# Three PNA layers of a graph network: batch norm folded into the mix weights, layer norm on ScalarE, the next head in groups of five blocks

## The chip, the cores and the metric

One core of one Trainium2 chip runs the kernel. The metric is the device time of one launch in microseconds (us), the median of three runs. Engines: PE (TensorE), DVE (VectorE), ACT (ScalarE), POOL (GpSimd), and SP, which here only issues DMAs.

## What is computed

A graph of N = 3125 nodes and 50000 edges, sorted by destination, with D = 128 features a node (float32), passes four parts: GCN, GIN, SAGE and three PNA layers, each part added to its input and layer-normed. The change lies in the PNA layers:

```python
def _pna_layer(h, src, dst, Mw, Mb, Uw, Ub, bn_g, bn_b, mix_w, mix_b):
    msg = jnp.concatenate([h[src], h[dst]], axis=-1) @ Mw.T + Mb
    ...            # sums of msg and msg*msg, max and min of msg over each node's edges
    agg = jnp.concatenate([mx, mn, std, var], axis=-1)
    ...            # h_neigh: agg, and agg scaled twice by the logarithm of the degree
    u = jnp.concatenate([h, h_neigh], axis=-1) @ Uw.T + Ub
    u = u * jnp.sqrt(1.0 / N)
    mu = jnp.mean(u, axis=0)
    v = jnp.mean((u - mu) ** 2, axis=0)
    u = (u - mu) / jnp.sqrt(v + BN_EPS) * bn_g + bn_b
    out = jax.nn.leaky_relu(u @ mix_w.T + mix_b, 0.01)
    return out + h
for l in range(3):
    h = _pna_layer(h, src_sl, dst_sl, Mw[l], ...)
    mu, v = ...    # mean and variance of each node's row
    h = jax.nn.elu((h - mu) / jnp.sqrt(v + LN_EPS) * ln_g[l] + ln_b[l])
```

## The kernel before

The nodes lie in NB = 25 blocks of 128, in NG = 5 groups of GB = 5 blocks; NCB = 7 banks hold four blocks each. There is no scheduler: each engine has its own program, written out by hand, in which every wait on a semaphore stands in its place, so the order on an engine is the order of the code. A layer runs like this.

**Head.** When a group of x is ready (s_grp), PE turns the blocks one by one (L1524) into two banks in turn, ACT copies each to ft2 or ft (L1318), PE multiplies it by M (L1621), DVE copies the result to g (L976). g is the part of the message that depends on the source node. Ahead of that, DVE writes the first four slots of source indices (L968). SP then writes g to DRAM as a_dram (L491, one DMA of 1600 KB) and starts two slabs of the count matrix (L456). DVE makes ft = g * g (L979) and splits g and ft into three bf16 parts each (L774 and L779, casts on ACT at L1211 and L1217).

**Loop.** POOL waits for a_dram and gathers rows by source index (L615): one gather per column of edges, four columns a slot (Q = 4), four slots (RING), so 16 in a batch. DVE runs the maximum and minimum over the columns (L1045, L1048), and writes the next indices for a slot when it has used it; between two batches it takes one block's share of PE's sums (L991 to L1024). SP writes the columns' state to scan_dram (L502). After the last column POOL gathers the ends of the segments from scan_dram (L632).

**U products, batch norm.** PE turns the ends and multiplies them by U (L1689, L1697), DVE adds up (L1112 to L1114), PE turns the result so that edge_sum holds u with features on the partitions (L1705), DVE takes statistics and makes cscale and cshift (L845 to L850).

**Mix.** For each block ACT makes turned = edge_sum * cscale + cshift (L1374), PE multiplies it by the mix weights (L1709) and adds the bias as a product of one row of ones with the bias row (L1710), ACT copies the bank to agg (L1379). A float32 product shows in the trace as a pair of passes. After a group DVE takes the leaky maximum (L1126), adds x (L1127) and takes row statistics (L1129); after all, L1132, the root on ACT (L1249) and rstd (L1135).

**Layer norm and ELU.** DVE subtracts the mean and multiplies by the first row of weights block by block (L1140), then by rstd and adds the second row (L1144). ACT makes exp(-relu(-y)) of a group in g (L1385, L1387); DVE takes max(y, 0) - 1 (L1151) and adds g, which gives x (L1152, s_grp). These two are one group behind. Weights of the next layer are loaded by SP as soon as the last use of the old ones is over (s_y). After the third layer x3 is reloaded (L521), added and normed (L828 to L837), and written out (L523, L525).

## Time and profile before

| | |
|---|---|
| median of three runs | 3907.63 us (3900.43 to 3912.53) |
| the profiled execution | 3915.32 us |
| its span | 3913.5 us |
| PE busy | 2472.3 us (63%) |
| DVE busy | 2233.6 us (57%) |
| POOL busy | 1258.7 us (32%) |
| ACT busy | 692.3 us (18%) |
| mean granted TensorE clock | 0.785 |

The span runs from the first to the last instruction that the profile shows; the execution's own time holds 1.8 us more. Busy times are of the whole span, whose last 2500 us, roughly, are the three PNA layers. The clock is given as a share of full speed (2.4 GHz).

### The profile page before, as it was taken

How to read it: one execution, taken by the hardware profiler on the slowest of the kernel's cores; microseconds unless marked ns; L12 is line 12 of the kernel's file. 1: busy time of each engine (PE TensorE's matmuls, PEld its weight loads, DVE VectorE, ACT ScalarE, POOL GpSimd, SP SyncE). 2: the span in 40 equal slices, each digit the busy share in tenths (PEclk: the TensorE clock that was granted, in tenths of full speed). 3: DMA queues.
4: the chain of work that ended last, by engine and by line, in shares of the span. 5: the costliest groups of instructions: out<-in, count | busy, mean ns of one | idle time of the engine just before them, and what ended most of it. 6: DMA issues, size and time to landing. Idle time of an engine off the chain costs nothing. (4 is left out here: it accounts for less than half of the span.)

```text
span 3913.5 us, 50857 instructions
## 1 busy us (share of the span) xinstructions
PE 2472.3 (63%) x11996; PEld 1384.5 (35%) x11997; DVE 2233.6 (57%) x6995; ACT 692.3 (18%) x1557; POOL 1258.7 (32%) x1321
## 2 busy tenths in 40 slices
PE   6988879886968955455456654454448644544563
PEld 2444345743635532222224422222225322222242
DVE  6877766463353265555555645555556645555555
ACT  0235532411121030000001500000003300000112
POOL 3000000002000036666642155655640356555520
PEclk8999989997979977677678676766767867767785
DMA  3122366253523535444441144444430444444411
GB/s 109 50 93 109 142 210 230 99 206 124 176 81 138 176 100 179 159 163 159 138 145 40 53 160 144 160 155 135 157 113 1 141 136 160 154 134 158 153 43 45
DMA packets 152225, 511.54 MB, mean 131 GB/s; under 512 B 32194, under 2 KB 51552, under 8 KB 151248
## 3 DMA queue, kind: packets, MB, share of 16 engines
q1 hardware_dynamic: 94782, 350.03, 25.5%
q0 software_dynamic: 43536, 93.43, 8.6%
q10 hardware_dynamic: 13826, 67.12, 4.2%
q8 instruction: 37, 0.61, 0.1%
q14 instruction: 44, 0.36, 0.0%
HBM read 280.33 MB, written 230.13 MB: 130 GB/s over the span
## 5 line engine op out<-in xcount | busy, mean ns | idle before, releaser
L615 POOL DMA_INDIRECT rows_g<-a_dram,idx_now x1173 | 1133.3, 966 | 1566.8 <-DMA a_dram<-g 801.4
L1485 PE MATMUL psum<-hs,slab 128*128 128x384 bf16 x6600 | 1196.2, 341 | 166.2 <-issue 124.0
L1485 PEld LDWEIGHTS psum<-hs,slab 128*128 128x128 bf16 x6600 | 674.5, 102 | 711.2 <-issue 326.3
L1045 DVE SCALAR_TENSOR_TENSOR run<-run,mask_pt,rows_g 128x128 f32<-128x128 f32 x1170 | 405.6, 347 | 278.5 <-issue 224.7
L1048 DVE SCALAR_TENSOR_TENSOR run<-run,mask_pt,rows_g 128x128 f32<-128x128 f32 x1170 | 403.3, 345 | 34.6 <-issue 26.8
L1637 PE MATMUL psum<-identity,std_now 128*128 128x128 f32 x75 | 33.6, 448 | 598.1 <-ACT std_now L1341 512.9
L1432 PE MATMUL psum<-onehot_key,onehot_lane 128*128 128x512 bf16 (+1 forms) x1968 | 366.4, 343 | 60.9 <-issue 36.3
L726 DVE TENSOR_SCALAR onehot_key<-key_row,key_at 128x1600 bf16<-128x1600 f16 x492 | 310.2, 630 | 0.0
L1644 PE MATMUL psum<-w_U,vturned 128*128 128x384 f32 x150 | 119.2, 896 | 292.6 <-ACT vturned L1349 265.2
L1341 ACT ACTIVATE std_now<-var_now,eps 128x128 f32<-128x128 f32 x75 | 30.1, 401 | 1444.5 <-DVE var_now L1007 928.9
L1432 PEld LDWEIGHTS psum<-onehot_key,onehot_lane 128*128 128x128 bf16 x1968 | 160.4, 100 | 249.5 <-issue 55.0
L1637 PEld LDWEIGHTS psum<-identity,std_now 128*128 128x128 f32 x75 | 13.2, 176 | 629.9 <-ACT std_now L1341 536.9
L804 DVE TENSOR_REDUCE agg<-psum 128x384 f32 (+1 forms) x125 | 69.5, 556 | 271.3 <-PE psum L1505 240.4
L725 DVE TENSOR_SCALAR onehot_lane<-lane_row,lane_at 128x128 bf16<-128x128 f16 x492 | 123.8, 252 | 103.3 <-PE psum L1432 86.1
L797 DVE SCALAR_TENSOR_TENSOR run<-run,var_tmp 128x128 f32<-128x128 f32 x391 | 137.4, 351 | 59.3 <-DVE run L797 15.7
L1644 PEld LDWEIGHTS psum<-w_U,vturned 128*128 128x128 f32 x150 | 36.3, 301 | 320.7 <-ACT vturned L1349 292.6
L603 POOL DMA_INDIRECT edge_sum<-sums_dram,end_idx x25 | 23.8, 953 | 388.6 <-DMA sums_dram<-run 381.3
L593 POOL PARTITION_ALL_REDUCE most<-most x1 | 0.4, 380 | 440.7 <-DVE most L744 440.7
L991 DVE TENSOR_REDUCE var_tmp<-psum 128x128 f32<-128x384 f32 x150 | 76.4, 551 | 76.7 <-remote 54.8
L1697 PE MATMUL psum<-w_U,turned 128*128 128x384 f32 x300 | 115.3, 509 | 0.1
L1185 ACT ACTIVATE part_now<-psum 128x1600 bf16<-128x1600 f32 x50 | 74.9, 1499 | 191.6 <-PE psum L1453 170.9
L1645 PE MATMUL psum<-w_U,vturned 128*128 128x384 f32 x150 | 107.2, 817 | 0.0
(298 smaller groups left out, 3018.2 us busy)
## 6 DMA issues: line engine op xcount, KB each, us to landing
slab<-at_part SPq DMA_DIRECT2D x200, 800.0 KB
scan_dram<-run SPq DMA_DIRECT2D x291, 512.0 KB
at_part<-part_now ACTq DMA_DIRECT2D x50, 800.0 KB, 3.6
sums_dram<-run ACTq DMA_DIRECT2D x43, 576.0 KB, 2.9
rows_g<-a_dram,idx_now POOLq DMA_INDIRECT x1173
rows_g<-in_attr SPq DMA_DIRECT2D x43, 148.5 KB
a_dram<-g SPq DMA_DIRECT2D x3, 1600.0 KB, 7.7
agg<-sel_dram SPq DMA_DIRECT2D x3, 1600.0 KB
```

Source lines behind the costliest of these rows:

```text
L615: nc.gpsimd.indirect_dma_start(rows_g[:, slot, j, :], None, a_dram, bass.IndirectOffsetOnAxis(ap=idx_now[:, slot, j:j + 1], axis=0)).then_ ...
L725: V.tensor_scalar(onehot_lane[:, j, :], lane_row[:], lane_at[:, ds(at, 1)], None, ALU.is_equal)
L726: V.tensor_scalar(onehot_key[:, j, :], key_row[:], key_at[:, ds(at, 1)], None, ALU.is_equal).then_inc(s_oh, 1)
L797: V.scalar_tensor_tensor(esum[:, slot, j, :], before, same[:, ds(EC * e + j, 1)], esum[:, slot, j, :], ALU.mult, ALU.add).then_inc(s_erun, 1)
L991: last = V.tensor_reduce(var_tmp[:, k, :], bank(2 + 2 * odd + k)[:, 0:3 * D].rearrange("p (s f) -> p f s", s=3), AX.X, ALU.add)
L1045: V.scalar_tensor_tensor(at[:, 0:D], before[:, 0:D], mark, rows, ALU.add, ALU.max).then_inc(s_run, 1)
L1048: V.scalar_tensor_tensor(at[:, D:2 * D], before[:, D:2 * D], mark, rows, ALU.subtract, ALU.min).then_inc(s_run, 1)
L1432: mm = T_.matmul(psum[:, 2048 * h + lo:2048 * h + hi], onehot_lane[:, j, :], onehot_key[:, j, lo:hi], start=(start and j == 0), stop=False ...
L1485: T_.matmul(ps[:, 0:3 * D], counts[:, k * P:(k + 1) * P], hs[:, k, at:at + 3, :].rearrange("p s f -> p (s f)"), start=(k == 0), stop=False ...
L1644: T_.matmul(bank(7)[:, 0:3 * D], vturned[:, 0:P], weights["U"][:, 2, :], start=True, stop=False)
L1645: T_.matmul(bank(7)[:, 0:3 * D], vturned[:, P:2 * P], weights["U"][:, 3, :], start=False, stop=True).then_inc(s_vmm, 1)
L1697: mm = T_.matmul(bank(2 + b % 2)[:, 0:3 * D], turned[:, b % 2, j * P:(j + 1) * P], weights["U"][:, j, :], start=(j == 0), stop=(j == 1))
```

## The change

It does four things.

- **Mix.** u * cscale + cshift, times the mix weights, is u times (cscale * weights), plus a row that is the same for all nodes. DVE scales the weights once (mix_now), PE makes cshift times the weights as one row, DVE adds the bias (mix_row). PE then multiplies edge_sum as it is, four blocks into a bank, and adds the row to the whole bank with one product of 512 columns. ACT writes 0.01 times the bank to agg, one operation a bank; DVE takes the maximum of that and the bank, adds x, and takes statistics.
- **Layer norm.** ACT normalizes each block (scale rstd, bias minus_mean); DVE multiplies and adds the two weight rows for a group of five blocks at once.
- **Head.** The next layer's transposes, copies and M products are done by groups of five blocks and written between the groups of the norm on all three engines (take_g, copy_xt). Layer 0 has them ahead of its loop. The first index slots are written ahead of the norm.
- **DMAs.** a_dram is written in five pieces, POOL waits for all of them. The weights of the next layer but M are loaded behind these and ahead of the slabs; those loads whose values no layer uses are left out.

```diff
+                for i in range(NG):
+                    sp.wait_ge(s_g, NG * l + i + 1)
+                    sp.dma_start(a_dram[GB * i * P:(GB * i + GB) * P, :].rearrange("(b p) f -> p b f", p=P),
+                                 g[:, GB * i:GB * i + GB, :]).then_inc(s_a_out, 16)
+                if l == 0:
+                    sp.wait_ge(s_x3, 16)
+                    sp.wait_ge(s_sel_out, 16)
+                else:
+                    sp.wait_ge(s_y, NG * l)
+                    layer_weights(LATER, l, s_lw)
                 load = counts(l + CALLS, 2)
                 load(0, 0, 0)
                 load(1, 1, 0)
...
-                layer_weights(["M"], (l + 1) % LAYERS, s_lm)
-                sp.wait_ge(s_y, NG * l + NG)
-                layer_weights(LATER, (l + 1) % LAYERS, s_lw)
+                if l + 1 < LAYERS:
+                    layer_weights(["M"], l + 1, s_lm)
...
-                pool.wait_ge(s_a_out, 16 * l + 16)
+                pool.wait_ge(s_a_out, 16 * NG * l + 16 * NG)
...
+            def take_g(l, i):
+
+                dve.wait_ge(s_gm, NG * l + i + 1)
+                at = 2048 + 1024 * (i % 2)
+                V.tensor_copy(flat(g)[:, GB * D * i:GB * D * (i + 1)], psum[:, at:at + GB * D]).then_inc(s_g, 1)
+
+            def first_indices(l):
+
+                if l:
+                    dve.wait_ge(s_run, 2 * T * l)
+                for k in range(RING):
+                    V.tensor_copy(idx_now[:, k, :], src_pt[:, Q * k:Q * k + Q]).then_inc(s_idx, 1)
+
+            def told_by(ins_):
+
+                made[0] += 1
+                ins_.then_inc(s_dve, 1)
+                return made[0]
+
+            first_indices(0)
+            for i in range(NG):
+                take_g(0, i)
...
-                if l:
-                    dve.wait_ge(s_run, 2 * T * l)
-                for k in range(RING):
-                    take_indices(0, k)
-                for b in range(NB):
-                    dve.wait_ge(s_mm, 3 * NB * l + MM3 + (b + 1))
-                    V.tensor_copy(g[:, b, :], bank(4 + b % 2)[:, 0:D]).then_inc(s_res, 1)
-                dve.wait_ge(s_res, 2 * NB * l + MM3 + NB)
+                dve.wait_ge(s_g, NG * l + NG)
...
                 batch_norm(lcols[:, 0:1], lcols[:, 1:2], S_LAYER * l + (S_X3 + 1))
-                for i in range(NG):
-                    at = slice(GB * i, GB * i + GB)
-                    dve.wait_ge(s_res, 2 * NB * l + (MM3 + NB + GB * i + GB))
-                    step(V.scalar_tensor_tensor(agg[:, at, :], agg[:, at, :], 0.01, agg[:, at, :], ALU.mult, ALU.max))
-                    step(V.tensor_tensor(agg[:, at, :], agg[:, at, :], x[:, at, :], ALU.add))
-                    for b in range(GB * i, GB * i + GB):
-                        last = V.bn_stats(stats[:, b, :], agg[:, b, :])
-                step(last)
+                V.tensor_scalar(mix_now[:], weights["mix"][:], cscale[:, 0:1], None, ALU.mult).then_inc(s_mix_now, 1)
+                dve.wait_ge(s_shifted, l + 1)
+                V.tensor_tensor(mix_row[:], bank(7)[0:1, 0:D], lrows[0:1, 2, :], ALU.add).then_inc(s_mix_row, 1)
+
+                def stats_of(j):
+                    for b in range(4 * j, min(NB, 4 * j + 4)):
+                        ins_ = V.bn_stats(stats[:, b, :], agg[:, b, :])
+                    return ins_
+
+                for j in range(NCB):
+                    at = slice(4 * j, min(NB, 4 * j + 4))
+                    rows, ps = agg[:, at, :], bank(j)[:, 0:(at.stop - at.start) * D].rearrange("p (b f) -> p b f", f=D)
+                    dve.wait_ge(s_leak, NCB * l + j + 1)
+                    leaky = told_by(V.tensor_tensor(rows, rows, ps, ALU.max))
+                    if j:
+                        stats_of(j - 1)
+                    dve.wait_ge(s_dve, leaky)
+                    added = told_by(V.tensor_tensor(rows, rows, x[:, at, :], ALU.add))
+                    dve.wait_ge(s_dve, added)
+                step(stats_of(NCB - 1))
                 for b in range(NB):
                     last = V.bn_aggr(mv[:, b, :], stats[:, b, :])
                 last.then_inc(s_rows, 1)
                 dve.wait_ge(s_std, S_LAYER * l + (S_X3 + 2))
                 step(V.reciprocal(rstd[:], std[:]))
-                for i in range(NG + 1):
+                V.scalar_tensor_tensor(minus_mean[:], mv[:, :, 0], -1.0, rstd[:], ALU.mult, ALU.mult).then_inc(s_rstd, 1)
+                if l + 1 < LAYERS:
+                    first_indices(l + 1)
+
+                def on_group(k):
+                    return lrows[:, k:k + 1, :].to_broadcast([P, GB, D])
+
+                for i in range(NG + 2):
+                    now, past = slice(GB * i, GB * i + GB), slice(GB * i - GB, GB * i)
                     if i < NG:
-
-                        for b in range(GB * i, GB * i + GB):
-                            last = V.scalar_tensor_tensor(agg[:, b, :], agg[:, b, :], mv[:, b, 0:1], lrows[:, 3, :],
-                                                          ALU.subtract, ALU.mult)
-                        step(last)
-                        for b in range(GB * i, GB * i + GB):
-                            last = V.scalar_tensor_tensor(agg[:, b, :], agg[:, b, :], rstd[:, b:b + 1],
-                                                          lrows[:, 4, :], ALU.mult, ALU.add)
-                        last.then_inc(s_y, 1)
-                    if i >= 1:
-
-                        at = slice(GB * i - GB, GB * i)
+                        dve.wait_ge(s_norm, NG * l + i + 1)
+                        scaled = told_by(V.tensor_tensor(agg[:, now, :], agg[:, now, :], on_group(3), ALU.mult))
+                    if 1 <= i <= NG:
                         dve.wait_ge(s_e, NG * l + i)
-                        step(V.tensor_scalar(agg[:, at, :], agg[:, at, :], 0.0, -1.0, ALU.max, ALU.add))
-                        V.tensor_tensor(x[:, at, :], agg[:, at, :], g[:, at, :], ALU.add).then_inc(s_grp, 1)
+                        upper = told_by(V.tensor_scalar(agg[:, past, :], agg[:, past, :], 0.0, -1.0, ALU.max, ALU.add))
+                    if i < NG:
+                        dve.wait_ge(s_dve, scaled)
+                        V.tensor_tensor(agg[:, now, :], agg[:, now, :], on_group(4), ALU.add).then_inc(s_y, 1)
+                    if 1 <= i <= NG:
+                        dve.wait_ge(s_dve, upper)
+                        V.tensor_tensor(x[:, past, :], agg[:, past, :], g[:, past, :], ALU.add).then_inc(s_grp, 1)
+                    if i >= 2 and l + 1 < LAYERS:
+                        take_g(l + 1, i - 2)
...
+            def copy_xt(l, i):
+
+                act.wait_ge(s_xt, NG * l + i + 1)
+                at = 1024 * (i % 2)
+                A.copy(ft2[:, GB * P * i:GB * P * (i + 1)], psum[:, at:at + GB * P]).then_inc(s_xc, 1)
+
+            for i in range(NG):
+                copy_xt(0, i)
...
-                act.wait_ge(s_rows, told(4))
-                for i in range(NB + 1):
-                    if i < NB:
-                        if i >= 2:
-                            act.wait_ge(s_mm, mms + (2 * NB + i - 1))
-                        A.activation(turned[:, i % 2, 0:D], edge_sum[:, i, :], ACT.Identity, bias=cshift[:, 0:1],
-                                     scale=cscale[:, 0:1]).then_inc(s_trc, 1)
-                    if i >= 1:
-                        b = i - 1
-                        act.wait_ge(s_mm, mms + (2 * NB + b + 1))
-                        A.copy(agg[:, b, :], bank(4 + b % 2)[:, 0:D]).then_inc(s_res, 1)
+                for j in range(NCB):
+                    at = slice(4 * j, min(NB, 4 * j + 4))
+                    act.wait_ge(s_mixed, NCB * l + j + 1)
+                    A.mul(agg[:, at, :], bank(j)[:, 0:(at.stop - at.start) * D].rearrange("p (b f) -> p b f", f=D),
+                          0.01).then_inc(s_leak, 1)
                 root_of(told(5), std[:], mv[:, :, 1], 0)
+                act.wait_ge(s_rstd, l + 1)
+
+                def normalize(i):
+
+                    for b in range(GB * i, GB * i + GB):
+                        last = A.activation(agg[:, b, :], agg[:, b, :], ACT.Identity, bias=minus_mean[:, b:b + 1],
+                                            scale=rstd[:, b:b + 1])
+                    last.then_inc(s_norm, 1)
+
+                normalize(0)
                 for i in range(NG):
-
+                    if i + 1 < NG:
+                        normalize(i + 1)
                     at = slice(GB * i, GB * i + GB)
                     act.wait_ge(s_y, NG * l + (i + 1))
                     A.activation(g[:, at, :], agg[:, at, :], ACT.Relu, scale=-1.0).then_inc(s_neg, 1)
                     act.wait_ge(s_neg, NG * l + (i + 1))
                     A.activation(g[:, at, :], g[:, at, :], ACT.Exp, scale=-1.0).then_inc(s_e, 1)
+                    if i >= 1 and l + 1 < LAYERS:
+                        copy_xt(l + 1, i - 1)
+                if l + 1 < LAYERS:
+                    copy_xt(l + 1, NG - 1)
...
+                for i in range(NG + 1):
+                    if i < NG:
+                        pe.wait_ge(s_grp, NG * l + (i + 1))
+                        if i >= 2:
+                            pe.wait_ge(s_xc, NG * l + (i - 1))
+                        for j in range(GB):
+                            at = 1024 * (i % 2) + j * P
+                            mm = T_.transpose(psum[:, at:at + P], x[:, GB * i + j, :], identity[:])
+                        mm.then_inc(s_xt, 1)
                     if i >= 1:
-                        b = i - 1
-                        pe.wait_ge(s_trc, trcs + (b + 1))
-                        if b >= 2:
-                            pe.wait_ge(s_res, ress + (b - 1))
-                        T_.matmul(bank(4 + b % 2)[:, 0:D], ft2[:, b * P:(b + 1) * P], weights["M"][:, 0:D],
-                                 start=True, stop=True).then_inc(s_mm, 1)
+                        k = i - 1
+                        pe.wait_ge(s_xc, NG * l + (k + 1))
+                        if k >= 2:
+                            pe.wait_ge(s_g, NG * l + (k - 1))
+                        for j in range(GB):
+                            at, b = 2048 + 1024 * (k % 2) + j * D, GB * k + j
+                            mm = T_.matmul(psum[:, at:at + D], ft2[:, b * P:(b + 1) * P], weights["M"][:, 0:D],
+                                          start=True, stop=True, skip_group_check=True)
+                        mm.then_inc(s_gm, 1)
+                pe.wait_ge(s_g, NG * l + NG)
...
-                def mixed(ps, t):
-                    T_.matmul(ps[:, 0:D], t, weights["mix"][:], start=True, stop=False)
-                    return T_.matmul(ps[:, 0:D], ones[0:1, :], weights["L3_rows"][0:1, 2, :], start=False, stop=True)
-
-                turned_products(None, 3 * NB * l + 7 * NB, 2 * NB * l + (MM3 + NB), mixed)
+                T_.matmul(bank(7)[0:1, 0:D], cshift[:], weights["mix"][:], start=True, stop=True).then_inc(s_shifted, 1)
+                pe.wait_ge(s_mix_now, l + 1)
+                for j in range(NCB):
+                    blocks = range(4 * j, min(NB, 4 * j + 4))
+                    for b in blocks:
+                        T_.matmul(bank(j)[:, (b - 4 * j) * D:(b - 4 * j + 1) * D], edge_sum[:, b, :], mix_now[:],
+                                 start=(b == 4 * j), stop=False, skip_group_check=True)
+                    if j == 0:
+                        pe.wait_ge(s_mix_row, l + 1)
+                    T_.matmul(bank(j)[:, 0:len(blocks) * D].rearrange("p (b f) -> p b f", f=D), ones[0:1, :],
+                             mix_row[:].unsqueeze(1).to_broadcast([1, len(blocks), D]), start=False, stop=True,
+                             skip_group_check=True).then_inc(s_mixed, 1)
```

PE, start of the mix stage (turned is ACT's result, w_L_rows the bias row). Before:

```order
L1705 MATMUL psum<-identity,u_row 128x128 [waits s_act,s_u] x2
L1709 MATMUL psum<-w_mix,turned 128x128 [waits s_trc,s_rows]
L1710 MATMUL psum<-w_L_rows,ones 128x128
L1709 MATMUL psum<-w_mix,turned 128x128 [waits s_trc]
L1710 MATMUL psum<-w_L_rows,ones 128x128
L1709 MATMUL psum<-w_mix,turned 128x128 [waits s_res,s_trc]
```

Now:

```order
L1780 MATMUL psum<-identity,u_row 128x128 [waits s_act,s_u] x2
L1782 MATMUL psum<-w_mix,cshift 1x128 [waits s_rows]
L1787 MATMUL psum<-mix_now,edge_sum 128x128 [waits s_mix_now]
L1787 MATMUL psum<-mix_now,edge_sum 128x128 x3
L1791 MATMUL psum<-mix_row,ones 128x512 [waits s_mix_row]
L1787 MATMUL psum<-mix_now,edge_sum 128x128 x4
L1791 MATMUL psum<-mix_row,ones 128x512
```

A bias product followed each block; now one follows four blocks, and no bank waits for a copy.

DVE, end of the norm and start of the next layer's head. Before:

```order
L1140 SCALAR_TENSOR_TENSOR agg<-agg,mv,w_L_rows 128x128 x5
L1144 SCALAR_TENSOR_TENSOR agg<-agg,rstd,w_L_rows 128x128 [waits s_dve]
L1144 SCALAR_TENSOR_TENSOR agg<-agg,rstd,w_L_rows 128x128 x4
L1151 TENSOR_SCALAR agg<-agg 128x640 [waits s_e]
L1152 TENSOR_TENSOR x<-agg,g 128x640 [waits s_dve]
L1151 TENSOR_SCALAR agg<-agg 128x640 [waits s_e]
L1152 TENSOR_TENSOR x<-agg,g 128x640 [waits s_dve]
L968 COPY idx_now<-src_pt 128x4 [waits s_run,s_grp]
L968 COPY idx_now<-src_pt 128x4 x3
L976 COPY g<-psum 128x128 [waits s_mm] x25
```

Now, from the third group of the norm on:

```order
L1194 TENSOR_TENSOR agg<-agg,w_L_rows 128x640 [waits s_norm]
L1197 TENSOR_SCALAR agg<-agg 128x640 [waits s_e]
L1200 TENSOR_TENSOR agg<-agg,w_L_rows 128x640 [waits s_dve]
L1203 TENSOR_TENSOR x<-agg,g 128x640 [waits s_dve]
L986 COPY g<-psum 128x640 [waits s_gm]
L1194 TENSOR_TENSOR agg<-agg,w_L_rows 128x640 [waits s_norm]
```

The 25 copies of g behind the norm have become five, the first three of them between the groups of the norm, each with a wait on PE; the ten small operations a group have become two large ones.

## Rows read from the trace of the kernel before

**Rows 1.** Windows, end of layer 0: span, each engine's busy time and count, clock, DMA

```profile
2151.00:2188.00 37.00, 35.59 (x100) 24.54 (x100) 11.23 (x31) 16.50 (x50) 0.00 (x0) 0.52 0.00 1
2214.00:2227.00 13.00, 12.71 (x73) 9.85 (x72) 7.53 (x30) 5.95 (x23) 0.00 (x0) 0.86 0.14 52
```

**Rows 2.** Timeline of DVE: start, length (us), operation, [idle before <- releaser]

```profile
1411.84 3.48 DVE L979 TENSOR_TENSOR ft<-g 128x3200 f32<-128x3200 f32 x1
...
2151.16 0.16 DVE L850 TENSOR_TENSOR cshift<-w_L_cols,cshift 128x1 f32<-128x1 f32 x1
...
2189.64 1.07 DVE L1129 BATCH_NORM_STATS2 stats<-agg 128x6 f32<-128x128 f32 x5
...
2192.88 0.32 DVE L1135 RECIPROCAL rstd<-std 128x25 f32<-128x25 f32 x1 [0.39 <-ACT std L1249]
...
2213.15 0.83 DVE L1152 TENSOR_TENSOR x<-agg,g 128x640 f32<-128x640 f32 x1
...
2227.04 3.48 DVE L979 TENSOR_TENSOR ft<-g 128x3200 f32<-128x3200 f32 x1
...
2282.47 1.02 DVE L991 TENSOR_REDUCE var_tmp<-psum 128x128 f32<-128x384 f32 x2 [17.79 <-remote]
```

**Rows 3.** Timeline of POOL and DVE, start of the loops of layers 1 and 2

```profile
2235.64 2.44 POOL L615 DMA_INDIRECT rows_g<-a_dram,idx_now  x1 [145.98 <-DMA a_dram<-g]
...
2245.87 2.74 DVE L779 TENSOR_TENSOR hs<-agg,hs 128x640 bf16<-128x640 f32 x3 [0.47 <-ACT hs L1217]
...
2277.29 0.94 POOL L615 DMA_INDIRECT rows_g<-a_dram,idx_now  x1 [0.30 <-issue]
...
3079.31 2.74 DVE L779 TENSOR_TENSOR hs<-agg,hs 128x640 bf16<-128x640 f32 x3 [0.47 <-ACT hs L1217]
...
3110.83 0.94 POOL L615 DMA_INDIRECT rows_g<-a_dram,idx_now  x1 [0.30 <-issue]
...
3115.86 1.02 DVE L991 TENSOR_REDUCE var_tmp<-psum 128x128 f32<-128x384 f32 x2 [18.43 <-remote]
```

**Rows 4.** Timeline of POOL: two batches of layer 1's loop, first gathers of the ends

```profile
2058.69 0.94 POOL L632 DMA_INDIRECT hs<-scan_dram,end_idx  x1 [26.61 <-DMA scan_dram<-run]
...
2500.55 0.94 POOL L615 DMA_INDIRECT rows_g<-a_dram,idx_now  x1 [7.01 <-DVE idx_now L968]
...
2526.74 0.94 POOL L615 DMA_INDIRECT rows_g<-a_dram,idx_now  x1 [6.37 <-DVE idx_now L968]
...
2893.02 0.94 POOL L632 DMA_INDIRECT hs<-scan_dram,end_idx  x1 [13.43 <-DMA scan_dram<-run]
```

**Rows 5.** Timeline of PE: passes of an earlier part, and layer 0's first transposes

```profile
682.27 0.42 PE L1524 MATMUL psum<-identity,agg 128*128 128x128 f32 x1
682.49 1.91 PE L1557 MATMUL psum<-turned,w_L_W1T 128*128 128x128 f32 x8
...
685.52 0.27 PE L1524 MATMUL psum<-identity,agg 128*128 128x128 f32 x1
685.63 1.06 PE L1557 MATMUL psum<-turned,w_L_W1T 128*128 128x128 f32 x8
...
1089.81 1.10 PE L1592 MATMUL psum<-ft,w_L_W 128*128 128x512 f32 x2 [0.28 <-DVE ft L926]
...
1397.41 0.69 PE L1524 MATMUL psum<-identity,x 128*128 128x128 f32 x2 [10.88 <-DVEq L767]
```

**Rows 6.** Timeline of ACT: the first two operations of the mix stage

```profile
2151.36 0.88 ACT L1374 ACTIVATE turned<-edge_sum,cshift,cscale 128x128 f32<-128x128 f32 x2 [0.81 <-DVE cshift L850]
```

**Rows 7.** Groups by line, 1750 to 3913: count | busy, mean ns | idle before

```profile
L1385 ACT ACTIVATE g<-agg 128x640 f32<-128x640 f32 x15 | 11.1, 737 | 32.9 <-DVE agg L1144 32.9
...
L1151 DVE TENSOR_SCALAR agg<-agg 128x640 f32<-128x640 f32 x15 | 7.3, 490 | 1.2 <-ACT g L1387 0.9
```

**Rows 8.** DMA issues, 2210 to 2250: count, KB each, median us to landing

```profile
a_dram<-g SPq DMA_DIRECT2D x1, 1600.0 KB, 7.7
...
w_L_rows<-in_L_rows SPq DMA_DIRECT2D x1, 320.0 KB, 4.3
```

More of the change, by code:

```diff
@@ L175, in gnn_kernel @@
         cshift = sb("cshift", [P, 1], F32)
+        mix_now = sb("mix_now", [P, D], F32)
+        mix_row = sb("mix_row", [1, D], F32)
+        minus_mean = sb("minus_mean", [P, NB], F32)
         eps = sb("eps", [P, 2], F32)
@@ L343, in gnn_kernel @@
         s_res = sem("s_res")
+        s_xt = sem("s_xt")
+        s_xc = sem("s_xc")
+        s_gm = sem("s_gm")
+        s_g = sem("s_g")
+        s_mix_now = sem("s_mix_now")
+        s_shifted = sem("s_shifted")
+        s_mix_row = sem("s_mix_row")
+        s_mixed = sem("s_mixed")
+        s_leak = sem("s_leak")
+        s_rstd = sem("s_rstd")
+        s_norm = sem("s_norm")
         s_hid = sem("s_hid")
@@ L525, in _ @@
             sp.dma_start(out[(NB - 1) * P:N, :], x[0:N - (NB - 1) * P, NB - 1, :]).then_inc(s_out, 16)
-            sp.wait_ge(s_lm, 16 * (LAYERS + 1))
-            sp.wait_ge(s_lw, 16 * len(LATER) * (LAYERS + 1))
+            sp.wait_ge(s_lm, 16 * LAYERS)
+            sp.wait_ge(s_lw, 16 * len(LATER) * LAYERS)
             sp.wait_ge(s_out, 32)
@@ L1313, in told @@
                     return V_LAYER * l + V_X3 + k
-                mms = 3 * NB * l + MM3
-                for b in range(NB):
-                    act.wait_ge(s_tr, 2 * NB * l + 4 * NB + (b + 1))
-                    A.copy(ft2[:, b * P:(b + 1) * P], bank(b % 2)[:, 0:P]).then_inc(s_trc, 1)
+                mms = NB * l + MM3
                 taken, turns = [0], [0]
@@ L1609, in _ @@
                 pe.wait_ge(s_lm, 16 * l + 16)
[L1610 to L1622 removed]
+                trcs = NB * l + 5 * NB
+                for i in range(NG + 1):
[7 more added lines that the diff above has]
+                        mm.then_inc(s_xt, 1)
+                    if i >= 1:
+                        k = i - 1
[8 more added lines that the diff above has]
+                pe.wait_ge(s_g, NG * l + NG)
                 for b in range(NB):
```

20 lines of the change are left out of this document (5 added, 15 removed).

## Prediction

> **What bounds the kernel now.** I read the page first. Its chain of waits covers only a few per cent of the span, so it can't say what a stage is worth. I cut the boundary between two layers of the last part into stretches instead [rows 1]: while the mix products run, PE is busy 35.6 of 37 us at a granted clock of 0.52; during the head of the next layer (transposes, M products) it is busy 12.7 of 13 us. Next I took DVE's timeline across the same boundary [rows 2]. The batch norm's shift is ready at 2151.3, the last statistics end at 2190.7, rstd at 2193.2, the last x at 2214.0, the last g at 2227.0. These stand behind one another: the reader should see three stages in series, 39.4, 20.8 and 13.0 us. They run on one path, once per layer.
>
> After g the path is less plain. DVE has 22 us of splits and then 18 us in which it waits at L991 until 2282.5 [rows 2]. POOL starts its gathers at 2235.6, when a_dram has landed, and runs 32 in a row to 2278.2; DVE goes on 4.2 us later. In the next layer the last of the 32 ends at 3111.8 and DVE goes on at 3115.9, 4.1 us later [rows 3]. In the loop the same shape returns: POOL pauses for 6 to 7 us after a batch of 16 gathers, and the batches start 26.2 us apart [rows 4]. So I take it that the loop hangs on POOL: what starts POOL earlier moves the layer. The splits have over 10 us of slack.
>
> **The mix products.** Before: 25 blocks, each a pair of passes for the product and a pair for the bias, 0.72 us a pair at the low clock (35.6 us for 100 passes) [rows 1]. Streams of 128-column passes without the change between 128 and 1 rows start 0.22 us apart at the low clock and 0.11 at the high one (682.27 to 682.49 and 685.52 to 685.63, and the runs of 8 behind them); a pair of 512 columns takes 1.10 less its last pass's end, 0.85, at the high clock, so 1.7 at the low [rows 5]. The change makes 25 product pairs and 7 bias pairs (six of 512 columns). Low clock: 4 x 0.44 + 1.7 + some 0.5 for two switches = 4.0 a bank, 25.4 in all. High clock: 2.2 a bank on PE, and now DVE sets the pace: the maximum and the sum over 512 elements (0.69 each, 0.83 being that of 640), four statistics 0.85 [rows 2] and waits give 2.4 a bank. With 0.5 us for the shift product and the row ahead, and about 2.1 us behind PE for the last bank, the stage takes 28.0 us low; high it is 0.5 + 2.2 + 0.6 (ScalarE's first bank) + 6 x 2.4 + 1.7 = 19.4. Against 39.4: **-11.4 or -20.0**. ScalarE's 50 small operations become 7 and are covered by PE.
>
> Which clock? Before, this stage stayed at 1.2 GHz for 36 us although PE was 96% busy; half of its passes feed one row. The head beside it, all on 128 rows, rose to 2.4 GHz within its 13 us (mean 0.86) [rows 1]. The new stage streams more densely, 43% of the time on 128 rows, and lies between. I take the middle, **-15.7**, and keep both ends.
>
> *A page against the row.* The Trainium skill (TensorE: Matmul & The Clock Gate, "What's actually happening") says the clock is set by how busy PE has recently been. By that the old stage should have run at full clock; its row says 0.52, and the measurement decides. If the page's rule were all there is, the new stage would rise and the high value would hold.
>
> **Norm, ELU and the next head.** Before, 20.8 + 13.0 = 33.8 us from rstd to g. Now ScalarE normalizes (5 x 0.39 a group, the pitch of the pair at L1374 [rows 6]), DVE scales and shifts whole groups (2 x 0.83), ELU's two steps 0.49 + 0.83 [rows 2, 7], and DVE then takes a head group (0.83) that waits for PE: five transposes of the group just finished and five products of the one before. That is a new wait, and queued behind it on DVE is the next group's scaling. PE's part is 3.6 us low (5 x 0.22 and 10 x 0.22, a start each) and 1.9 high. A full round is 3.0 + 0.8 + 3.6 + 0.1 = 7.5 us low, 5.8 high. I walked the three engines through: the first g group is taken 16.3 us (14.6) after rstd, the next ones start at 23.8 (20.3), 31.2 (26.0), 37.1 (30.2), 39.4 (31.4), end 40.3 (32.2). With 0.3 for the negated mean: 40.6 or 32.5, **+6.8 or -1.3**. PE now has short bursts with pauses, so neither clock is sure: middle +2.8. ScalarE (1.95 + 0.74 + 0.74 [rows 7] + 0.7 = 4.1 a group, and one table load) stays under the round. So the overlap gives nearly nothing: ScalarE and PE trade with DVE in turn.
>
> **a_dram in five pieces.** Before, 1600 KB land after 7.7 us [rows 8] and POOL starts 8.7 us after the last g [rows 2, 3]. Now only 320 KB are left. Bounds: a 320 KB load behind 768 KB took 4.3 us [rows 8]; a fifth of 7.7 is 1.5. With 1.0 for the way to POOL I take 3.5, nearest to the proportion: **-5.2** (-3.4 to -6.2). POOL's 17th gather needs the indices that DVE makes after the first columns, 23.6 us after g; POOL would want them 3.5 + 20.4 = 23.9 after g, so just in time. The weights of the next layer move on SP's queue from before the head to behind the five pieces and ahead of the two slab loads; even at a landing time of 4.3 us [rows 8] for that queue they hide behind the 22 us of splits.
>
> **Layer 0 and the end.** Layer 0's head took 14.4 us, 1397.4 to 1411.8 [rows 5, 2]. Nothing else is in its way now; PE's five groups need 11.3 us (low for the first 4.5), the last copy 0.9: -2, and -5.2 for POOL: **-7.2**. The last layer has no head: the norm loses 1.3 us (22.1 for 20.8: group 1's ELU waits for two normalizations and the table), the mix gains 15.7, and the weights that nobody uses no longer precede the load of x3, 0.5: **-14.9**.
>
> **Sum.** Two boundaries at -15.7 + 2.8 - 5.2 = -18.1, so -36.2; -14.9; -7.2: **-58.3 us**. The profiled execution is 3915.3 us, 7.7 above the median of 3907.6; the sum gives 3857 there and **3850** against the median. The indices at the loop's start, the new row and column tiles and the semaphores are hidden (DVE's four copies lie beside ScalarE's first group); without that cover 0.4 us a layer.
>
> **Rivals.**
> - *Clock high in both stages* (busy is enough). -20.0 - 1.3 - 5.2 = -26.5 twice, -19.2, -7.2 = -79: 3828. For it: the denser stream. Against: 36 us at 0.52. The rule of the Trainium skill's page above would give this outcome; the trace disagrees so far.
> - *Clock low in both*. -9.8 twice, -10.6, -7.2 = -37: 3870. For it: the row-poor bias passes stay 1.7 us long.
> - *POOL's start isn't what the loop waits for.* DVE goes on 33.9 us after the splits' end in layer 1 and 33.8 in layer 2 [rows 2, 3], which fits as well as POOL's 4.2 and 4.1. Then the three 5.2 are not gained: 3865. Against it: in the loop each batch of POOL is followed by the same release.
> - *Slower: the loop's period grows.* From g to the first gather of the ends, layer 0 takes 646.9 us and layer 1 666.0 [rows 2, 4], with the same code and idle time that the profile calls issue: 19.1 us, 0.8 for each of 24 batches. The change moves all code behind it. One more such step in every layer costs layer 0 38.2 us and the others 19.1 each, 76.4 in all: 3926. It decides from there: below 70 us (1.0 a batch over 72) the result is no slower than before. The other way, layers 1 and 2 at layer 0's pace give 3812.
> - *The change doesn't do what it says*: DVE blocked at the first g group could stall more than I walked. At +29 us a boundary it cancels the gain; each of four rounds would have to take some 15 us instead of 7.5.
>
> **Chances.** Forecast 0.40, high clock 0.16, low clock 0.16, POOL not the bound 0.12, short loops 0.05, long loops 0.07, cancelled 0.04; each spills a little over its edge. The likeliest gives 3850; 3815 to 3890 takes in both clocks and the two ends of the a_dram price. A measurement of this kernel tells about 0.3% (12 us) from no change; faster 0.87, same 0.05, slower 0.08.
>
> **What would show it.** In the profile after: the mix stage 19 to 28 us from shift to last statistics, its clock above 0.52 where the middle holds; copies of g at DVE five times a layer with a wait on PE of 2 to 4 us before each; POOL starting 3 to 4 us after the last of them; DVE's release at L991's successor 46 to 47 us after POOL's start; the batches 25 to 26.5 us apart. I am wrong if the release stays 34 us behind the splits while POOL starts earlier, if POOL's batches drift apart, or if the rounds exceed 8 us.

## The result, and the profile after

| | before | after |
|---|---|---|
| median | 3905.24 us (3900.43 to 3912.53, 4 runs) | 3847.77 us (3835.11 to 3856.43, 4 runs) |
| ratio, 95% interval | | 0.9851 (0.983 to 0.9871) |
| span of the profiled execution | 3913.5 us | 3854.6 us |
| PE / DVE / ACT / POOL busy | 2472.3 / 2233.6 / 692.3 / 1258.7 us | 2450.6 / 2204.9 / 673.8 / 1263.9 us |
| mean granted TensorE clock | 0.785 | 0.785 |

The change takes 57.5 us off the median; 3850 was forecast. The spans differ by 58.9 us, the sum of the prediction was 58.3. So good an agreement of totals has to be checked stage by stage.

Timeline of DVE after the change, from the end of layer 0 on (start, length, operation, [idle before <- releaser]):

```profile
2142.16 0.16 DVE L869 TENSOR_TENSOR cshift<-w_L_cols,cshift 128x1 f32<-128x1 f32 x1
...
2170.33 1.76 DVE L1179 BATCH_NORM_AGGREGATE mv<-stats 128x2 f32<-128x6 f32 x25
2172.47 0.32 DVE L1182 RECIPROCAL rstd<-std 128x25 f32<-128x25 f32 x1 [0.39 <-ACT std L1302]
...
2188.42 0.82 DVE L986 COPY g<-psum 128x640 f32<-128x640 f32 x1 [3.43 <-PE psum L1694]
2189.16 0.81 DVE L1194 TENSOR_TENSOR agg<-agg,w_L_rows 128x640 f32<-128x640 f32 x1
2189.89 0.49 DVE L1197 TENSOR_SCALAR agg<-agg 128x640 f32<-128x640 f32 x1
2190.30 0.82 DVE L1200 TENSOR_TENSOR agg<-agg,w_L_rows 128x640 f32<-128x640 f32 x1
2191.03 0.82 DVE L1203 TENSOR_TENSOR x<-agg,g 128x640 f32<-128x640 f32 x1
2195.27 0.82 DVE L986 COPY g<-psum 128x640 f32<-128x640 f32 x1 [3.42 <-PE psum L1694]
...
2209.91 3.48 DVE L1014 TENSOR_TENSOR ft<-g 128x3200 f32<-128x3200 f32 x1
...
2259.27 1.02 DVE L1026 TENSOR_REDUCE var_tmp<-psum 128x128 f32<-128x384 f32 x2 [15.42 <-remote]
```

These answer to [rows 2]. Shift to last statistics took 28.0 us (39.4 before), rstd to the end of the head 37.1 (33.8 before), and a round between two copies of g lasts 6.85 us, of which DVE waits 3.4 for PE. Windows of the mix stage, of norm and head, and of two stretches in one round of it, between PE's work and during it (columns as in [rows 1]):

```profile
2142.00:2168.00 26.00, 24.95 (x66) 13.94 (x66) 11.77 (x35) 3.86 (x7) 0.00 (x0) 0.53 0.00 1
2172.80:2209.90 37.10, 16.02 (x76) 14.89 (x77) 18.28 (x31) 21.41 (x41) 0.00 (x0) 0.66 0.11 35
2189.00:2191.80 2.80, 0.00 (x0) 0.00 (x0) 2.80 (x5) 1.33 (x3) 0.00 (x0) 0.95 0.37 117
2191.80:2195.30 3.50, 3.33 (x15) 3.13 (x15) 0.08 (x2) 1.51 (x3) 0.00 (x0) 0.55 0.00 0
```

The mix stage is shorter, and PE is still busy 96% of the time at the low clock. In the norm the mean of 0.66 misleads: the clock was high between PE's bursts (0.95, no pass) and low while it worked (0.55). Timeline of PE, one bank and one round of the head:

```profile
2143.77 2.07 PE L1791 MATMUL psum<-mix_row,ones 1*128 1x512 f32 x2
2145.77 2.08 PE L1787 MATMUL psum<-mix_now,edge_sum 128*128 128x128 f32 x8
...
2191.91 1.33 PE L1685 MATMUL psum<-identity,x 128*128 128x128 f32 x5 [3.52 <-DVE x L1203]
2193.03 2.20 PE L1694 MATMUL psum<-w_M,ft 128*128 128x128 f32 x10
```

Half of a bank's 4.0 us is the product that feeds a single row. In the head's round PE needs 1.1 + 2.2 us after DVE's x, which is DVE's wait of 3.4. Timeline of POOL, first and 32nd gather of layer 1, one pause of its loop:

```profile
2213.34 0.94 POOL L634 DMA_INDIRECT rows_g<-a_dram,idx_now  x1 [132.58 <-DMA a_dram<-g]
...
2254.90 0.95 POOL L634 DMA_INDIRECT rows_g<-a_dram,idx_now  x1 [0.31 <-issue]
...
2527.04 0.94 POOL L634 DMA_INDIRECT rows_g<-a_dram,idx_now  x1 [6.24 <-DVE idx_now L1010]
```

POOL starts 3.4 us behind the last g (8.6 in [rows 3]), and DVE goes on 3.4 us after POOL's 32nd gather (4.2 before), though now only 27.7 us behind the splits (33.9 before).

The whole span, cut at the same events in all profiles; sums over the layers, in us. "Ahead" is all code before the PNA layers, "g to release" runs from the last copy of g to the end of DVE's wait for the first count products (L991, now L1026), "loop" from there to the first gather of the ends.

| stage | before | after | difference | forecast |
|---|---|---|---|---|
| ahead | 1397.4 | 1402.1 | +4.7 | 0 |
| head of layer 0 | 14.4 | 11.6 | -2.8 | -2.0 |
| g to release, 3 layers | 166.2 | 150.0 | -16.2 | -15.6 |
| loop, 3 layers | 1812.1 | 1795.1 | -17.0 | 0 |
| ends, U products, batch norm | 276.0 | 276.3 | +0.3 | 0 |
| mix stage, 3 layers | 119.2 | 84.7 | -34.5 | -47.1 |
| norm and head, 2 boundaries | 72.5 | 79.6 | +7.1 | +5.6 |
| norm of layer 2 | 23.2 | 23.5 | +0.3 | +1.3 |
| end | 32.4 | 31.7 | -0.7 | -0.5 |

Two terms missed: the mix stage gave 12.6 us less than forecast, and the loops gave 17.0 us that nobody had put down. Together with the 4.7 ahead of the layers, where nothing was changed, they cancelled.

### The profile page after: what moved, and what is told of

It is laid out like the page before. It is cut to its first block and busy times, and to the rows that moved or that the text cites. A ratio compares the mean times of both kernels' runs of the same rounds, so it can differ in the third digit from the quotient of the medians.

```text
span 3854.6 us, 50270 instructions
## 1 busy us (share of the span) xinstructions
PE 2450.6 (64%) x11894; PEld 1364.3 (35%) x11895; DVE 2204.9 (57%) x6836; ACT 673.8 (17%) x1443; POOL 1263.9 (33%) x1321
## 5 line engine op out<-in xcount | busy, mean ns | idle before, releaser
L1719 PE MATMUL psum<-w_U,vturned 128*128 128x384 f32 x150 | 117.7, 886 | 390.1 <-ACT vturned L1407 356.5
L1712 PEld LDWEIGHTS psum<-identity,std_now 128*128 128x128 f32 x75 | 12.6, 168 | 493.8 <-ACT std_now L1399 399.9
L1026 DVE TENSOR_REDUCE var_tmp<-psum 128x128 f32<-128x384 f32 x150 | 76.3, 550 | 67.2 <-remote 47.2
L1407 ACT COPY vturned<-psum 128x256 f32<-128x256 f32 x75 | 27.9, 373 | 459.7 <-remote 385.4
```

Of the source, the lines that this page charges most:

```text
L1026: last = V.tensor_reduce(var_tmp[:, k, :], bank(2 + 2 * odd + k)[:, 0:3 * D].rearrange("p (s f) -> p f s", s=3), AX.X, ALU.add)
L1719: T_.matmul(bank(7)[:, 0:3 * D], vturned[:, 0:P], weights["U"][:, 2, :], start=True, stop=False)
```

## Experiments

The experiments ran on three chips, each time beside the kernel before on the same chip, and the chips differ: 3383.1, 3894.8 and 3952.6 us for the same kernel. So a median is compared on its own chip alone, and stages are compared across chips only where the stage doesn't depend on the chip. I call the chips A (3383.1), B (3894.8) and C (3952.6).

### Chip A: the changed kernel once more

> The changed kernel, unaltered, once more. If the time between the first release of the count products and the first gather of the ends (586.6, 600.7 and 607.8 us in the three layers of the first profile) belongs to the program, it comes back within 2 us a layer here; if it varies from execution to execution, layers move by 5 us or more, and the 17.1 us that the loops gained against the kernel before are partly chance. The median should lie within 3835 to 3856 either way.

Measured: 3336.1 us, ratio 0.9859 (0.9844 to 0.9874). My bound on the median fell at once: the program took 512 us less on this chip. The change gains 47.0 us here. That is close to the 46.5 that the stages in the table above give without the loops and the part ahead. Mix stages (86.5 us in all) and the norm with the head (78.5) took what they took before; the loops took 1437.0 us instead of 1795.1. PE, SP and DVE at the start of layer 1's loop, and POOL in the loop:

```profile
2053.35 0.49 PE L1572 MATMUL psum<-hs,slab 128*128 128x384 bf16 x2
2053.67 6.50 PE L1552 MATMUL psum<-hs,slab 128*128 128x384 bf16 x39
```

```profile
2053.91 0.34 SPq L470 DMA_DIRECT2D slab<-at_part  x1
```

```profile
2054.91 1.01 DVE L1026 TENSOR_REDUCE var_tmp<-psum 128x128 f32<-128x384 f32 x2
```

```profile
2255.79 1.01 POOL L634 DMA_INDIRECT rows_g<-a_dram,idx_now  x1 [0.30 <-issue]
```

Here DVE doesn't wait at L1026 (it comes 12 us before POOL's 32nd gather has ended), and POOL never pauses: its batches of 16 start 20.2 to 20.5 us apart. In the profile after, the same places of PE's and SP's programs read so:

```profile
2241.95 0.49 PE L1572 MATMUL psum<-hs,slab 128*128 128x384 bf16 x2
...
2244.42 0.32 PE L1552 MATMUL psum<-hs,slab 128*128 128x384 bf16 x1 [1.08 <-issue]
2245.83 0.32 PE L1552 MATMUL psum<-hs,slab 128*128 128x384 bf16 x1 [1.08 <-issue]
...
2257.02 0.48 PE L1552 MATMUL psum<-hs,slab 128*128 128x384 bf16 x1 [1.61 <-issue]
...
2258.42 4.08 PE L1552 MATMUL psum<-hs,slab 128*128 128x384 bf16 x12 [0.20 <-issue]
```

```profile
2259.31 0.34 SPq L470 DMA_DIRECT2D slab<-at_part  x1
```

PE crawls, most passes 1.4 to 2.1 us behind the one before, waiting for nothing that the profile shows, and runs at full speed again 2.6 us after POOL's 32nd gather has ended (2255.85). But these passes aren't what DVE waits for. DVE (L1026) and SP (L470) wait for one semaphore, s_spmm, which the last pass of the first block raises (L1572), and that pass ended at 2242.4, ahead of the crawl. On chip A SP goes on 0.07 us after it; here SP and DVE go on together 16.8 us after it. In all ten profiles from the slower chips the trace has this semaphore's step 15 to 25 us behind the pass that makes it, and in the four from chip A 0.02 us. So DVE's release does follow POOL, and what it is late by lies between PE's pass and the semaphore; how POOL's gathers bring that about is not shown.

### Chip A: the old mix stage

The changed kernel with before's L1374, L1709, L1710 and L1379, and DVE's operations of before (L1126 to L1129), in place of mix_now, mix_row and the seven banks:

```diff
-                    T_.matmul(bank(j)[...], edge_sum[:, b, :], mix_now[:], start=(b == 4 * j), stop=False, ...)
+                    T_.matmul(bank(4 + b % 2)[:, 0:D], turned[:, b % 2, 0:P], weights["mix"][:], start=True, stop=False)
+                    T_.matmul(bank(4 + b % 2)[:, 0:D], ones[0:1, :], weights["L3_rows"][0:1, 2, :], start=False,
+                             stop=True).then_inc(s_m2, 1)
```

> The changed kernel with the mix stage of before (ScalarE scales and shifts block by block, a bias product a block). If the mix stage is worth what the first profile shows of it, 11.4 us in each of three layers, it takes 34 us more than the changed kernel, some 3882, and its stage 39.4 to 40 us. The rival: part of this gain is given back behind the stage (clock or weights arriving late), then it is below 25 us more.

Measured: 3367.1 us, 31.0 more than the changed kernel; its three mix stages took 119.7 us against 86.5. 37 us of the first one (windows, columns as in [rows 1]):

```profile
1944.00:1981.00 37.00, 36.21 (x100) 24.95 (x100) 10.95 (x29) 16.24 (x50) 0.00 (x0) 0.50 0.00 0
```

So the mix stage is worth its 11 us a layer (33.2 in the three stages, 31.0 in the median) and gives next to nothing back behind it.

### Chip A: a bias product of 128 rows

```diff
-                    T_.matmul(bank(j)[:, ...], ones[0:1, :], mix_row[:].unsqueeze(1).to_broadcast([1, ...]), ...)
+                    T_.matmul(bank(j)[:, ...], first_row[:], mix_row[:].unsqueeze(1).to_broadcast([P, ...]), ...)
```

first_row is 128x128, ones in its first row and zeros below; mix_row now has 128 rows, all but the first zero.

> The changed kernel with each bank's bias as a product of 128 rows (ones in the first, zeros in the rest) in place of one of a single row: the same passes and columns, the same result. If the passes that feed one row keep the clock low, the clock of the stage rises in its course, banks go from 4.0 to 2.4 us, the stage from 28.0 to 20 to 24, and it takes 12 to 24 us less. If the clock doesn't depend on the rows fed, the stage stays at 28.0 us and 0.52, and the time is the same.

Measured: 3304.7 us, 31.3 less than the changed kernel, and the stage takes 18.5 to 18.6 us in each layer: both better than I had expected. Windows from the start of the first mix stage:

```profile
1941.90:1946.00 4.10, 4.04 (x15) 2.79 (x16) 0.48 (x3) 0.32 (x1) 0.00 (x0) 0.60 0.00 0
1946.00:1951.00 5.00, 5.00 (x29) 3.61 (x28) 3.91 (x9) 1.48 (x3) 0.00 (x0) 0.98 0.01 3
```

With the same passes and columns, the clock stays at 0.50 when the bias products feed one row and rises in the second bank when they feed 128. PE's timeline stands below, from the kernel that has this part too.

### Chips A and C: a_dram in one piece

```diff
-                for i in range(NG):
-                    sp.wait_ge(s_g, NG * l + i + 1)
-                    sp.dma_start(a_dram[GB * i * P:(GB * i + GB) * P, :]..., g[:, GB * i:GB * i + GB, :]).then_inc(s_a_out, 16)
+                sp.wait_ge(s_g, NG * l + NG)
+                sp.dma_start(a_dram.rearrange("(b p) f -> p b f", p=P), g[:]).then_inc(s_a_out, 16)
```

> The changed kernel with a_dram written by one DMA after the last g. If the five pieces are what starts POOL early, POOL starts 8.6 us after the last g instead of 3.4, the release of DVE follows by the same 5.2, and it takes 3 x 5 = 15 to 18 us more. If the early start only came from the weight loads that were moved, it takes no more than 5 us more. If the release hangs on the end of the splits, POOL starts late and DVE is still released 27.7 us behind the splits.

> The changed kernel with a_dram in one piece again, now perhaps on a chip where PE's count products stall while POOL gathers. There the theory that POOL sets DVE's release says: POOL starts 8.5 us after the last g, DVE is released 3.4 to 4.2 us after the end of POOL's 32nd gather, 33 us and more behind the splits, and the kernel takes 15 us more. The rival (the release hangs on the end of the splits) says 27.7 us behind the splits and no more time.

Measured: on chip A 3354.0 us, 17.9 more than the changed kernel; on chip C 3905.1 us, 18.0 more than its 3887.1. Chip C, layer 1, in one piece:

```profile
2217.33 3.48 DVE L1012 TENSOR_TENSOR ft<-g 128x3200 f32<-128x3200 f32 x1
```

```profile
2225.94 2.43 POOL L632 DMA_INDIRECT rows_g<-a_dram,idx_now  x1 [138.83 <-DMA a_dram<-g]
...
2267.82 0.95 POOL L632 DMA_INDIRECT rows_g<-a_dram,idx_now  x1 [0.30 <-issue]
```

```profile
2273.26 1.02 DVE L1024 TENSOR_REDUCE var_tmp<-psum 128x128 f32<-128x384 f32 x2 [19.31 <-remote]
```

POOL starts 8.6 us behind g, DVE is released 4.5 us behind the 32nd gather and 34.3 behind the splits; with five pieces, on the same chip, it was 3.5, 4.0 and 28.1. The release went with POOL's start: the splits' end is not what it hangs on. SP also issued its loads of weights and slabs 4 us later, but PE didn't wait for them: its count products start 2.6 us behind the splits in both kernels. Over three layers g to release is 167.2 us against 150.4 on this chip.

### Chip B: DVE's copy of g one round later

```diff
-                for i in range(NG + 2):
+                for i in range(NG + 3):
...
-                    if i >= 2 and l + 1 < LAYERS:
-                        take_g(l + 1, i - 2)
+                    if i >= 3 and l + 1 < LAYERS:
+                        take_g(l + 1, i - 3)
```

> The changed kernel with DVE's copy of a head group one round later (i >= 3 in place of i >= 2), nothing else. In the first profile DVE waits 3.4 us for PE before each of three such copies while ScalarE waits 4.0 us for DVE. If that wait is what makes a round 6.85 us, a round falls to 4.5 to 5.5 us, rstd to last g from 37.1 to 29 to 33 us, and it takes 8 to 16 us less over the two boundaries. If PE or ScalarE is the bound of a round, nothing moves.

Measured: 3811.6 us, ratio to before 0.9777 (0.9757 to 0.9797), 25.0 us less than the shifted kernel (two sections below), which stands in for the changed one on this chip; the boundaries explain 21.4 of that. DVE:

```profile
2171.78 0.82 DVE L1203 TENSOR_TENSOR x<-agg,g 128x640 f32<-128x640 f32 x1
2172.51 0.82 DVE L986 COPY g<-psum 128x640 f32<-128x640 f32 x1
2173.24 0.82 DVE L1194 TENSOR_TENSOR agg<-agg,w_L_rows 128x640 f32<-128x640 f32 x1
...
2182.78 3.48 DVE L1014 TENSOR_TENSOR ft<-g 128x3200 f32<-128x3200 f32 x1
```

The wait before the copy is gone, a round lasts 3.9 to 4.2 us, and rstd to the end of the head is 26.6 us instead of 37.1 to 37.5: 10.7 us a boundary against the shifted kernel's 37.3, more than I expected. This comparison of stages is the firmer one: the medians also hold what the loops differ by, 12.0 us in the two profiles.

### Chip B: the head behind the norm

```diff
-                    if i >= 2 and l + 1 < LAYERS:
-                        take_g(l + 1, i - 2)
+                for i in range(NG if l + 1 < LAYERS else 0):
+                    take_g(l + 1, i)
```

and copy_xt on ScalarE in the same way.

> The changed kernel with the next head's copies on DVE and ScalarE behind the whole norm instead of between its groups (PE's program untouched). If the overlap of the change gives nothing, as the walk said, rstd to last g is 33 to 38 us as with it (21 for the norm, 12 to 16 for the head), and the time is within 8 us of the changed kernel. If the overlap hides the head, this takes over 20 us more.

Measured: 3821.0 us, 15.6 less than the shifted kernel beside it, out of the 8 us that I allowed; here too part of the median is loops (13.1 us in the profiles). DVE:

```profile
2173.52 0.83 DVE L1203 TENSOR_TENSOR x<-agg,g 128x640 f32<-128x640 f32 x1
2176.13 0.82 DVE L986 COPY g<-psum 128x640 f32<-128x640 f32 x1 [1.79 <-PE psum L1692]
...
2184.94 3.48 DVE L1014 TENSOR_TENSOR ft<-g 128x3200 f32<-128x3200 f32 x1
```

Norm 21.0, head 10.6, together 31.3 to 31.6 us: the overlap as the change has it costs 6 us a boundary against no overlap at all. Grouping by five blocks is what shortens the head, not the overlap.

### Chips B and C: code moved by 16 instructions

```diff
+            for k in range(16):
+                pe.sem_inc(s_pad[2], 1)
```

and the same on DVE and ScalarE, once ahead of the three layers.

> The changed kernel with 16 increments of an unused semaphore on each of PE, DVE and ScalarE once ahead of the three layers: 1 to 2 us of work, and all code behind it 16 instructions further on. If the pace of the loops depends on where their code lies, some of the three loop times (586.6, 600.7, 607.8 us) move by 5 us or more and stay so in both directions; if not, all three return within 2 us and the time is 1 to 2 us more.

> The kernel with 16 increments ahead of the layers again. Its loops took 580.2, 609.6 and 604.8 us. If they return within 3 us (on a chip of the same kind) while the changed kernel's return to 586.6, 600.7 and 607.8, the place of the code sets them and the 17.1 us that the loops gained are a matter of place; if they don't return, they are chance.

> The kernel before, unaltered, for a second profile. Its three loops (release of the count products to first gather of the ends) took 591.4, 610.6 and 610.2 us in the first one. If their pace belongs to the program and its place in memory, they return within 3 us on a chip of the same kind; if it is a matter of chance in each execution, they move by 5 us or more. On a chip of the kind of the second call of runs but one, where the whole takes 3383 us, they take some 480 us each.

> The changed kernel, unaltered, beside the other three of this call. On a chip where it takes about 3840 us: program and place say loops of 586.6, 600.7 and 607.8 us again, within 3 us; chance says that they move by 5 us or more. On a chip where it takes about 3336 us: 478 to 482 us each.

Measured: 3836.6 us on chip B; on chip C 3889.0, beside 3887.1 for the changed kernel and 3952.3 for the kernel before (before again: ratio 0.9996). The loops of the three layers, in us:

| kernel | first chip | B | C |
|---|---|---|---|
| before | 591.4, 610.6, 610.2 | | 599.1, 620.7, 624.9 |
| after | 586.6, 600.7, 607.8 | | 596.6, 614.2, 620.8 |
| shifted | | 580.2, 609.6, 604.8 | 590.1, 623.9, 620.2 |
| late copy | | 579.9, 597.7, 605.1 | |
| head behind norm | | 579.9, 598.7, 602.9 | |
| a_dram in one piece | | | 590.6, 614.5, 623.9 |
| late copy, 128 rows | | 579.8, 604.5, 606.8 | |

No loop returned within 3 us on another chip, because the chips differ by 8 to 15 us a loop; that part of my expectations couldn't be tested so. What can be compared is kernels on one chip. On C, with 16 instructions that do nothing, the loops differ by -6.5, +9.7 and -0.6 us; the longer second loop is there on B as well, 609.6 against 597.7 to 604.5 in kernels whose loops have the same code. But a_dram in one piece, which leaves the programs of PE, DVE and ScalarE as they are, differs by -6.0, +0.3 and +3.1, and the medians of the changed and the shifted kernel on C are 1.9 us apart, where executions of one kernel spread over 23 us. So one profile for each kernel and chip can't part place from chance, and no effect of place on the loops is shown. One small effect of the edit did come back: in layer 2 POOL starts 4.5 to 5.2 us behind g in every kernel with five pieces but two: the old mix has 3.5, and so have both profiles of the shifted kernel.

Is the gain of the loops real? Before to after is -4.8, -9.9, -2.4 on the first chip and -2.5, -6.5, -4.1 on C, 17 and 13 us in all. The medians say something like it: the stages without the loops and the part ahead give 46.5 and 46.7 us on these chips, and the medians differ by 57.5 and 65.5, so 11 and 19 us are left, each give or take 8. On chip A, where there is no profile of before, 47.0 less the same 46.5 leaves 0.5, give or take 5 (all estimates, from the medians' intervals). So it looks as if the loops gain on the slower chips only, where PE and DVE have the idle time that the profile calls issue. Why they gain is open. I thought of engines that fetch the code of their loops late. The Trainium skill (Runtime: NRT & Kernel Launch, "Instruction fetch mechanics") says that a taken branch to a page of instructions that isn't at hand forces a fetch by DMA and stalls the engine. The trace doesn't agree for PE's crawl: its gaps stand before single passes of a straight run of 48, not behind a branch, and in these 15.4 us (2243.0 to 2258.4 in the profile after) the only queue that moved anything is that of POOL's gathers, none of the two queues that carry instructions:

```profile
q0 software_dynamic: 369, 0.73, 17.8%
```

### Chip B: late copy and 128 rows together

> The changed kernel with DVE's copy of g one round later and with bias products of 128 rows. If both theories hold, the gains add up: 20 to 40 us less than the changed kernel, about 3815. If the clock doesn't rise, only the 8 to 16 us of the later copy remain.

Measured: 3792.1 us, ratio to before 0.9731 (0.971 to 0.9753), 44.5 less than the shifted kernel, a little more than expected. In the stages the gains add up: against the shifted kernel the mix stages take 30.3 us less in all and the two boundaries 21.5. PE in the first mix stage, and windows of that stage:

```profile
2131.21 1.41 PE L1796 MATMUL psum<-mix_row,first_row 128*128 128x512 f32 x2
2132.46 1.05 PE L1792 MATMUL psum<-mix_now,edge_sum 128*128 128x128 f32 x8
2133.35 1.02 PE L1796 MATMUL psum<-mix_row,first_row 128*128 128x512 f32 x2
2134.21 1.05 PE L1792 MATMUL psum<-mix_now,edge_sum 128*128 128x128 f32 x8
```

```profile
2128.80:2133.00 4.20, 4.18 (x17) 3.03 (x18) 0.44 (x2) 0.34 (x1) 0.00 (x0) 0.62 0.00 0
2133.00:2138.00 5.00, 5.00 (x30) 3.57 (x29) 4.24 (x10) 1.54 (x4) 0.00 (x0) 1.00 0.02 3
```

The clock is low at first and full from the second bank on. PE needs 1.75 us a bank instead of 4.0; DVE is now the one that sets the pace, with 2.1. The stage takes 18.4 to 19.3 us.

## Why the prediction was right, and where it wasn't

**Mix stage, wrong by 12.6 us.** The walk was right: 28.0 us at the low clock was forecast and measured, to the tenth, and 18.4 to 19.3 were measured for the stage at the high one, where 19.4 had been worked out. The step that failed is the middle: "The new stage streams more densely, 43% of the time on 128 rows, and lies between." It stayed at 0.53, as the old one at 0.52. I had the likely cause in hand, half of the passes feed one row, and didn't follow it: in the new stage such passes still hold half of PE's time, and with them on 128 rows the clock rose and the stage fell to 18.5 us. PE was 96% busy at 0.53, and went to the full clock with the same passes on 128 rows. The page's rule (the Trainium skill, TensorE: Matmul & The Clock Gate, "What's actually happening") goes by how busy PE is; as far as the profile's busy time tells that, these rows don't agree with it, and the rival that stood on it has lost its ground. The weight should have gone to the row that was nearest in kind, [rows 1], a stage with single-row passes, and not between it and the head.

**Norm and head, right, in part by luck.** 36.6 us forecast, 37.1 and 37.5 measured; DVE's wait of 3.4 us before each copy of g is the "2 to 4 us" of the text. But 36.6 was the middle between two clocks, and during the rounds' work PE had the low one (ten passes in 2.20 us), for which the walk had 40.6. The walk's round was too long, 7.5 us for 6.85: DVE's five operations take 3.43 us, since each begins before the one ahead has ended, where 3.8 was added up, and PE's part 3.4 where it was 3.7. So two errors met. That the overlap gives nearly nothing was too kind to it: against the same groups without overlap it costs 6 us a boundary.

**a_dram in five pieces, right.** 5.2 us a layer forecast; 5.9, 6.0 and 4.2 measured, and 16.8 us in all when the pieces are undone on chip C. The tie to POOL is shown on chips of this kind, by what way is open (chip A, above); the rival (the splits) has fallen. In layer 2 POOL starts 5.1 us behind g instead of 3.4, and 3.5 in the shifted kernel; why is open. On chip A, where DVE doesn't wait for POOL's 32nd gather, the pieces are worth the same 17.9 us, because POOL runs without a pause there (its batches start 20.3 to 20.5 us apart with and without the pieces) and every us of its start moves the end.

**Layer 0's head and the last layer, right** to 1 us each (-2.8 for -2.0, +0.3 for +1.3, -0.7 for -0.5).

**The loops, not in the sum.** The prediction had them as rivals of both signs, 0.8 us for each batch; what happened is smaller, 0.1 to 0.4 us a batch, with a cause that is open. A term of "0, give or take 15 us" would have been fairer. The loops made good what the mix stage lacked, so the total was near by luck: without the loops, the stages give 41.9 us less, not 58.9. **Ahead of the layers**, where nothing was changed, profiles of the first chip, B and C lie between 1389.9 and 1402.1 us; the +4.7 is of that scatter, and without it too the stages give 46.5.

## What to carry to other kernels

Price a PE stage by the clock that it will get, and look for products that feed one row: a bias row put into a 128-row product with zeros costs no more passes and here took the stage from 28 to 18.5 us. When work of two stages is interleaved in hand-written programs, try taking each result a round later than it can be ready at the earliest; a copy that waits for PE in the middle of DVE's program stops everything behind it. Ask what the clock was while PE worked: a mean over a stretch also counts its pauses. And cut the span at the same events in all profiles before a total is called explained.

## What the runs showed of the hardware that was not expected

The same kernel takes 3383.1 us on one chip and 3894.8 to 3952.6 on others, and most of the difference lies where POOL's gathers run beside loops of the other engines: between chips A and C the spans of the changed kernel differ by 546.4 us, of which 394.6 are the three loops (1437.0 against 1831.6) and 48.6 g to release; 63.5 lie in ends, U products and batch norm, 40.7 ahead of the layers. On the slower chips PE and DVE show gaps of 1 us and more marked issue while POOL gathers; on the faster one DVE's stay below 0.8 us and PE's crawl is missing, although the DMA engines are busier (0.91 against 0.52 in these 25 us):

```profile
2231.00:2256.00 25.00, 14.15 (x61) 6.54 (x62) 9.74 (x37) 1.28 (x1) 19.05 (x20) 0.73 0.52 161
```

```profile
2043.00:2068.00 25.00, 23.67 (x131) 13.73 (x132) 16.86 (x62) 2.71 (x4) 18.91 (x21) 0.93 0.91 294
```

The first is layer 1's start of the loop in the profile after, the second the same place on chip A (columns as in [rows 1]): 20 gathers in the one and 21 in the other, and PE ran 61 passes against 131. What makes the chips differ is open; no run could ask it.
